# Moving one key projection ahead of the first attention round, in a kernel of two cross-attentions and two feed-forward blocks

## The reference

```
x = x + xattn0(layernorm(x), ctx)          # 16 heads of 16, softmax, clip at 1e-12
x = x + ffn0(layernorm(x))                 # FP4-rounded weights and inputs, silu(gate) * up, width 704
x = x + xattn1(layernorm(x), ctx, mask)    # 16 heads of 64, masked softmax
x = x + ffn1(layernorm(x))                 # width 1024, piecewise linear gelu, values rounded to 1/256
```

## Time and profile before

| | |
|---|---|
| median of 3 runs | 940.83 us (940.82 to 941.83) |
| the profiled execution's time | 940.82 us |
| its span, first to last instruction | 939.0 us |
| PE busy | 900.3 us, 96% |
| DVE busy | 668.9 us, 71% |
| ACT busy | 601.4 us, 64% |
| POOL busy | 204.0 us, 22% |

### The profile page before, as it was taken

The page is one execution under the profiler, slowest core; times in us unless marked ns, Lnnn a source line. Parts: engine busy times, 40 slices in busy tenths (PEclk is TensorE's granted clock), DMA queues, the critical chain, the costliest instruction groups (busy, mean ns, idle before and its releaser), DMA issues.

```text
span 939.0 us, 16084 instructions
## 1 busy us (share of the span) xinstructions
PE 900.3 (96%) x5546; PEld 592.0 (63%) x5546; DVE 668.9 (71%) x2179; ACT 601.4 (64%) x1671; POOL 204.0 (22%) x316
## 2 busy tenths in 40 slices
PE   5999999999999999999999999999999999999998
PEld 2555564767665565577675566567757565647686
DVE  5999872763889785475598978267478988827568
ACT  3887425972789643795378943399257984269735
POOL 3211001762000000476000000077400000028500
PEclk9999999999999999999999999999999999999999
DMA  9500000000000010000000000000000000000000
GB/s 294 205 1 2 29 0 23 2 1 1 1 1 24 2 27 23 1 1 2 0 1 12 14 29 1 23 1 1 1 1 1 19 7 0 1 1 2 1 1 23
DMA packets 14560, 18.35 MB, mean 20 GB/s; under 512 B 3088, under 2 KB 11664, under 8 KB 14480
## 3 DMA queue, kind: packets, MB, share of 16 engines
q1 hardware_dynamic: 12288, 15.40, 5.0%
q10 hardware_dynamic: 2064, 1.91, 0.7%
q0 software_dynamic: 128, 0.01, 0.0%
HBM read 15.21 MB, written 2.10 MB: 18 GB/s over the span
## 4 chain that ended last, share of the span: by engine, by line
PE 70%; DVE 16%; ACT 9%; issue 4%; POOL 1%; DVEq 0%; POOLq 0%
PE bank L1233 28%; PE bank L1248 9%; PE bank L1484 6%; PE bank L1560 6%; PE bank L1464 5%; PE bank L1339 4%; PE bank L1396 4%; ACT ring L667 4%; DVE row_max L1040 3%; PE bank L1373 3%; ACT ring L709 2%; ACT ring L552 1%; PE bank L1530 1%; PE bank L1412 1%; DVE block_max L826 1%
## 5 line engine op out<-in xcount | busy, mean ns | idle before, releaser
L459 POOL TENSOR_TENSOR rstd<-var_eps,minus_half 128x2 f32<-128x2 f32 x32 | 23.4, 734 | 538.2 <-DVE var_eps L878 538.2
L477 POOL TENSOR_TENSOR ring<-ring,row_inv 128x256 f32<-128x256 f32 x192 | 112.2, 613 | 101.9 <-DVE row_inv L1135 101.9
L552 ACT ACTIVATE ring<-bank 128x512 f32<-128x512 f32 x224 | 123.5, 612 | 14.6 <-PE bank L1248 13.2
L1248 PE MATMUL bank<-ident_s,ring 128*128 128x128 f32 x768 | 104.8, 279 | 3.9 <-POOL ring L477 2.3
L1248 PEld LDWEIGHTS bank<-ident_s,ring 128*128 128x128 f32 x768 | 82.5, 141 | 37.9 <-issue 16.4
L709 ACT ACTIVATE ring<-ring,row_max 128x256 f32<-128x256 f32 x192 | 95.1, 497 | 17.3 <-DVE row_max L1128 17.3
L667 ACT ACTIVATE ring<-bank,row_max 128x256 f32<-128x256 f32 x192 | 88.4, 496 | 4.0 <-DVE row_max L1040 4.0
L1128 DVE CUSTOM_DVE_ANT_0 ring<-bank,maskbias 128x256 f32<-128x256 f32 x192 | 70.7, 420 | 23.4 <-issue 23.4
L1040 DVE TENSOR_REDUCE row_max<-bank 128x2 f32<-128x512 f32 x128 | 79.3, 682 | 4.4 <-PE bank L1373 3.7
L1233 PE MATMUL bank<-wgu_s,act_s 128*128 128x352 f32 x256 | 78.4, 459 | 0.0
L1233 PE MATMUL bank<-ctxT_s,wk_s 128*128 128x512 f32 x160 | 76.1, 599 | 0.7 <-DVE v L1026 0.7
(11 more groups left out here) (186 smaller groups left out, 1691.5 us busy)
## 6 DMA issues: line engine op xcount, KB each, us to landing
x_s<-x SPq DMA_DIRECT2D x4, 512.0 KB, 3.9
ctxT_s<-ctxT SPq DMA_DIRECT2D x4, 512.0 KB, 3.8
w_s<-w SPq DMA_DIRECT2D x2, 1024.0 KB, 16.2
out<-act_s SPq DMA_DIRECT2D x16, 128.0 KB, 1.7
wk_s<-wk SPq DMA_DIRECT2D x1, 1024.0 KB, 13.6
wv_s<-wv SPq DMA_DIRECT2D x1, 1024.0 KB, 15.0
wq_s<-wq SPq DMA_DIRECT2D x1, 1024.0 KB, 16.5
wo_s<-wo SPq DMA_DIRECT2D x1, 1024.0 KB, 16.9
```

What stands on the lines that cost most here:

```text
L477: ins = pool.tensor_tensor(probs1[i % PRING1][:, a, :], probs1[i % PRING1][:, a, :], row_inv[:, i, a:a + 1].to_broadcast([P, SEQ]), ALU.mult)
L552: act.activation(probsT[u % TRING][:, :, :].rearrange("p a q -> p (a q)"), psum(at, key)[:], ACT.Copy).then_inc(drain(at, key), 1)
L1248: ins = pe.transpose(psum(at, key)[:, c * SEQ + a * P:c * SEQ + (a + 1) * P], tile[:, a, c * P:(c + 1) * P], ident_s[:])
```

## The change

At the three seams key chunk 0 of the second attention moves. On PE it is computed right after `last_out` of chunks 6 and 7, before the transposes of units 0 and 1, in place of after the scores of round 1. It goes into bank 5 and no longer into bank 7; in bank 5 it takes its turn between the first attention's values of the same pass and the transposes of unit 1. On ACT its copy comes between the exponentials of units 1 and 2, in place of between the copies of the second and third unit's transposes. The other seven chunks and the opening pass stay as they are.

```diff
+KEYS_AHEAD = 1
@@ jobs_layer0
     if with_last_layer:
         jobs_last_out(jobs)
+        for m in range(KEYS_AHEAD):
+            jobs.add(("k1", m), 5)
@@
     for r in range(1, ROUNDS0 + 1):
-        jobs.add(("k1", r - 1), 7)
+        if not with_last_layer or r > KEYS_AHEAD:
+            jobs.add(("k1", r - 1), 7)
@@ ACT, layer0_heads
                         first = 4 * (r - 1)
-                        key_first = with_weights or r > 1
-                        if key_first:
+                        if with_weights or r > KEYS_AHEAD:
                             layer1_key(at, r - 1)
                         for i in (first, first + 1):
                             evacuate_probsT(at, 0, i)
-                        if not key_first:
-                            layer1_key(at, r - 1)
@@
                     if r < ROUNDS0:
                         for i in round_units0(r):
+                            if r == 0 and i == 2 and not with_weights:
+                                layer1_key(at, KEYS_AHEAD - 1)
                             exponentials(i)
@@ PE, layer0_heads
-                    key_first = with_weights or r > 1
-                    if r <= ROUNDS0 and key_first:
+                    if r <= ROUNDS0 and (with_weights or r > KEYS_AHEAD):
                         layer1_key(at, r - 1)
@@
                             layer0_scores(at, r)
-                            if not key_first:
-                                layer1_key(at, r - 1)
@@ PE, the seams
                 last_out(crossings[g], g, range(6, FC1))
+                for m in range(KEYS_AHEAD):
+                    layer1_key(crossings[g], m)
                 layer0_heads(crossings[g], g + 1, False)
```

## The result

The changed kernel takes 946.0 us (median of 5 runs, 944.95 to 946.4) against 940.83 us before (5 runs, 940.43 to 941.83): ratio 1.0056, 95% interval 1.0045 to 1.0067. The forecast was 945.6 us. The profiled execution took 946.27 us, its span is 944.5 us. The record has 22 executions of the changed kernel in all; their times go from 944.85 to 948.39 us, with a median of 946.26 us.

The account below looks back on a forecast made before the run. TensorE, busy 96% of the span, was taken to set the pace nearly everywhere. Three seams at 1.61 us add 4.83 us to 940.8, forecasting 945.6 us; own range 943.1 to 947.4, widened to 942.8 to 948.0.

Parts of the forecast that it names:

- What sets the pace: At the seams TensorE is busy without a break, so moving the key product there was taken to win 0 us.
- the five pieces: TensorE's transposes 0 and 1, scores, first key product, transposes 2 and 3, second key product: 6.82 us in either order.
- 1.16 - 0.87 = 0.29 us: Upper bound per seam on TensorE's waiting within the first pair of transposes, hence on the move's gain.
- ScalarE's wait: At each seam ScalarE stands still before the moved key copy, from 263.65 to 266.60: 2.95 us.
- The scores: Round 1's scores wait for the late exponentials, starting at 269.17 instead of 265.74; TensorE idles over 1 us.
- Given back or not: Weighted sums after each seam start 1.61 us late, and later rounds give none of it back.
- The sum: Three seams by 1.61 us add 4.83 us to 940.8 us, giving 945.6 us.
- The 0.6 us for later wake-ups: Allowance per seam for later wake-ups in the handovers, raising 1.61 to 2.2 us and the range's top to 947.4.
- Not slower: Rival: the key product fills a TensorE hole at the seams, -0.29 us each, 939.9 us or 939.1; chance 0.04.
- Only the bank wait costs: Rival: only the second unit's transposes wait for bank 5, 0.4 us a seam, 942.0 us; chance 0.05.
- It compounds: Rival: ScalarE's 3.44 us lateness per seam is not compensated, as late copies hold the transposes' banks; 951.1 us; chance 0.05.
- the clock: TensorE's clock falling in the new hole of under 1.4 us: not counted as a case, no price or chance.

Follow-up runs that it names:

- e5: The kernel before, without the first key product of each seam and its copy: 938.86 us against 942.11 us for the kernel before beside it, ratio 0.9966.
- e2: The changed kernel with the key product ahead of output products 6 and 7, copy left in place: 941.0 us against 941.93 us for the kernel before, ratio 0.9988.
- e4: The kernel before with only each seam's first key product put into bank 5 instead of 7: 943.62 us against 942.11 us, ratio 1.0014.
- e1: The changed kernel with ScalarE's key copy moved behind the exponential of unit 3: 942.44 us against 942.11 us for the kernel before, ratio 1.0007.
- e3: The changed kernel with the key copy one unit earlier, before the exponential of unit 1: 950.24 us against 942.11 us for the kernel before, ratio 1.0084.

## Why the prediction was right

**What sets the pace.** Right. In this stretch TensorE had no idle time and the five pieces only changed places; e5 shows that the moved product was paid for in full but for 0.5 us of 1.82.

Two readings around it were off. I bounded the gain by 1.16 - 0.87 = 0.29 us, a pair of transposes followed by scores against one followed by a key product. Followed by scores too, the pair of the next round takes 1.02 us to the next start in the kernel before (273.27 to 274.29), and e2's first pair 0.97, so at most 0.19 us was to be had there. In the changed kernel it can't be had, since ScalarE stands still. And I wrote that nothing is seen today of the scores' wait for the exponentials. The scores start 265.74 - 265.59 = 0.15 us after the last read of unit 3, which is the step that the earlier trace rows give for a start released by an exponential (0.14 us); e4 and e5 have 0.14 us at the same place. So in the kernel before the scores already start when the exponentials let them, though no idle time is printed. There was no slack: whatever holds ScalarE up in front of unit 3 delays the scores at once.

**ScalarE's wait.** Forecast 2.95 us, measured 2.73. Of the difference 0.1 us is the step from the product's start to the copy, 2.02 us by the earlier trace rows and 267.37 - 265.45 = 1.92 us now; the rest is that I counted from the second unit's next start, and the row counts from the end of its last read.

**The scores.** Forecast to start 0.14 us after the last read of unit 3, and over 1 us of idle time for TensorE. Measured 0.15 and 1.20 us. e1 and e3 move this step alone, to 0 and by another 0.9 us.

**Given back or not.** Forecast 1.61 us a seam whole, measured 1.53. The weighted sums start 8.31 us after the output products where I had 8.43; of the 0.12 us, 0.1 is the shorter step to the copy. VectorE keeps 0.18 us of its wait for the next exponential, where I had some 0.2. The next round is again gapless and takes 6.70 us, against 6.71.

**The sum.** 4.83 us forecast, 4.57 measured at the seams. The medians of five differ by 5.2, and the profiled executions by 4.57 and the 0.87 us of the opening. That the forecast of 945.6 us came within 0.4 us of the median is therefore luck in part: a seam was taken 0.08 us too dear, and the opening, which no part of the forecast is about, made up for it. The 0.6 us for later wake-ups, with which the range was drawn upwards, is shown by no run: the steps came out at 1.92 us for 2.02 and 0.15 for 0.14.

**The rivals.** "Not slower" needed the product to be filled before ScalarE came to the copy. I saw no way to that within the change; e2 makes one by moving the product further, and is then faster by 0.31 us a seam. That this is the rival's price of 0.29 is a coincidence: only 0.19 us of it is the pair of transposes on which the price rests. "Only the bank wait costs" named a wait that exists (0.34 us), but it is not what ends last. "It compounds" did not happen in the changed kernel; e3 adds a loss of another kind, by the clock and not by the banks that I had named. I set the clock aside because a 1.84 us wait had left it alone. The conclusion held for the changed kernel's holes and not for e3's. The reason was weaker than I took it for: it rested on one execution, and in the traces of e1 and e5 the clock is lower behind that very wait (last section).

## What to carry to other kernels

Moving a product earlier on one engine moves its copy forward on another, and in an in-order list what counts is whether the product is filled when the copy's turn comes; if not, everything behind the copy inherits the wait. An idle time that is off the chain, such as ScalarE's 2.27 us, is not a gain to be collected: ask what would stand behind the wait in its new place. When an early result is wanted, move the producer until it is ready before the consumer's turn, then the consumer. And where no idle time is printed in front of a group, compare its start with the end of the work that it depends on before calling that work early.

## What the runs showed of the hardware

**The clock and holes.** In the changed kernel TensorE's two holes (0.34 and 1.20 us) left the granted clock at 1.00 in all three seams of the trace. In e3, where it was busy 1.25 of 3.67 us, with transposes only, the clock fell to the 1.2 GHz level for part of what follows in the first seam (mean 0.66 and 0.77), and in the second seam too (0.50 from 501 to 504 us), but not in the third, with 1.26 of 3.68 us busy and a clock of 1.00 before and behind. So the same hole cost extra in two passes of three; no run here shows what decides it.

**The opening.** Runs of one kernel differ by 1 to 3 us (the kernel before from 940.43 to 943.61). The traces, one of each kernel, show differences of that size ahead of the first seam, in code that is the same in all. The eight warm-up matmuls take 5.13 to 6.54 us in the eight traces; before, then after:

```profile
6.78 5.54 PE L1567 MATMUL bank<-v 128*128 128x512 f32 x8 [6.78 <-POOL two L449]
```

```profile
6.78 6.38 PE L1566 MATMUL bank<-v 128*128 128x512 f32 x8 [6.78 <-POOL two L453]
```

This is the 0.87 us (0.85 of it) by which the changed kernel is late at the first group already. The granted clock reads 1.00 in both there, and what makes the warm-up longer stays open. In two of the eight traces more is added behind the 1.84 us wait of the earlier trace rows: in e1 and e5 the first values' product takes 5.41 us where it takes 3.72 before, with a mean granted clock of 0.66 from 25 to 30 us. This is e1's row:

```profile
24.93 5.41 PE L1236 MATMUL bank<-wv_s,ctxT_s 128*128 128x256 f32 x16
```

So the same wait that left the clock alone in the profile before can be followed by a lower one in another execution. That the spread of the times of one kernel comes from here is likely but not shown, as each kernel has one trace. Effects under 2 us are better read from the period between two equal points of one trace than from medians.
